# The last 1024 tokens' projection moved into the first windows of the attention, and the first maxima beside the sixth group

## The reference

```python
xn = _layernorm(x)                                   # (1, 4096, 256)
Q, K, V = heads(xn @ W_Q), heads(xn @ W_K), heads(xn @ W_V)   # 16 heads of 16
scores = einsum('bhqd,bhkd->bhqk', Q, K) / 16 ** 0.5 + causal
out = einsum('bhqk,bhkd->bhqd', softmax(scores), V) ... @ W_o
x = x + out + ffn(xn)     # scores of 16 experts by gate_w, each takes its best 512 tokens,
                          # gelu(Wg x) * (Wu x) @ Wd, times the weight, added up; and a shared expert
```

## Time and profile before

| | |
|---|---|
| median of 3 runs | 2411.45 us (2410.39 to 2411.78) |
| profiled execution | 2411.44 us, its span 2409.7 us |
| PE busy | 2318.2 us, 96% |
| DVE busy | 1927.6 us, 80% |
| ACT busy | 1493.8 us, 62% |
| units' reductions on DVE (L954) | x2176, 1292.9 us |
| mean granted clock of TensorE | 0.974 |

### The profile page before, as it was taken

One profiled execution on the slowest core, in us unless ns is written; L12 is line 12 of the kernel. 1 busy time (PEld: TensorE's weight loads), 2 busy tenths in 40 slices (PEclk: granted clock), 3 DMA queues, 4 the chain that ended last, 5 costly groups with the idle time before them and its releaser, 6 DMA issues. The chain is left out here.

```text
span 2409.7 us, 52756 instructions
## 1 busy us (share of the span) xinstructions
PE 2318.2 (96%) x20269; PEld 1504.9 (62%) x20275; DVE 1927.6 (80%) x3721; ACT 1493.8 (62%) x2901; POOL 241.9 (10%) x228
## 2 busy tenths in 40 slices
PE   7987999999999999999999999998998999999997
PEld 4554555555555555555545555557887888888886
DVE  6776999999999898999999999865744666666664
ACT  2233677788877777888788877773223555455543
POOL 3000000000000000000002000001120232323232
PEclk9956999999999999999999999999999999999999
DMA  7854000003100004200001000002243444444444
GB/s 262 321 154 89 17 10 8 6 11 63 28 3 11 18 14 90 42 17 13 3 9 41 4 4 4 30 7 84 71 159 104 109 136 136 107 112 135 137 104 115
DMA packets 141914, 167.97 MB, mean 70 GB/s; under 512 B 53612, under 2 KB 107372, under 8 KB 141628
## 3 DMA queue, kind: packets, MB, share of 16 engines
q1 hardware_dynamic: 127916, 142.87, 19.4%
q0 software_dynamic: 13728, 22.28, 5.0%
q10 hardware_dynamic: 64, 0.02, 0.0%
HBM read 117.86 MB, written 48.56 MB: 69 GB/s over the span
## 5 line engine op out<-in xcount | busy, mean ns | idle before, releaser
L954 DVE TENSOR_REDUCE a_mp<-a_pm 128x1 f32<-128x512 f32 (+3 forms) x2176 | 1292.9, 673 | 78.3 <-PE a_pm L1121 54.2
L1079 ACT ACTIVATE a_p<-a_ps 128x512 f32<-128x512 f32 (+2 forms) x2176 | 1121.3, 587 | 373.5 <-PE a_ps L1202 266.0
L1224 PE MATMUL a_po<-a_p,a_v 128*32 128x384 f32 (+2 forms) x8688 | 615.1, 386 | 0.9
L1121 PE MATMUL a_pm<-a_k,a_qr 48*128 48x512 f32 (+3 forms) x1152 | 418.2, 459 | 3.1 <-ACT p_xs L379 1.2
L1202 PE MATMUL a_ps<-a_qr,a_k 50*128 50x512 f32 (+3 forms) x1152 | 390.0, 435 | 21.4 <-DMA a_qr<-a_nb 21.4
L1121 PE MATMUL a_pm<-a_k,a_q 48*128 48x512 f32 (+3 forms) x1152 | 405.0, 435 | 5.2
L1202 PE MATMUL a_ps<-a_q,a_k 50*128 50x512 f32 (+3 forms) x1152 | 372.8, 423 | 1.0 <-ACT a_p L1079 0.8
L1224 PEld LDWEIGHTS a_po<-a_p,a_v 128*32 128x32 f32 x8688 | 202.7, 109 | 202.3 <-issue 134.3
L1202 PEld LDWEIGHTS a_ps<-a_qr,a_k 50*128 50x128 f32 x1152 | 192.7, 192 | 198.1 <-ACT a_p L1079 143.4
L1202 PEld LDWEIGHTS a_ps<-a_q,a_k 50*128 50x128 f32 x1152 | 185.5, 185 | 185.0 <-ACT a_p L1079 161.2
L1644 ACT ACTIVATE e_g<-e_pg 128x512 f32<-128x512 f32 x128 | 76.5, 598 | 243.7 <-PE e_pu L1722 243.7
(11 more groups left out here) (177 smaller groups left out, 2052.8 us busy)
## 6 DMA issues: line engine op xcount, KB each, us to landing
e_wgu<-in_wg SPq DMA_DIRECT2D x18, 1024.0 KB, 5.6
e_wgu<-in_wu SPq DMA_DIRECT2D x18, 1024.0 KB, 7.6
e_wd<-in_wd SPq DMA_DIRECT2D x18, 1024.0 KB, 10.2
q_parts<-p_parts SPq DMA_DIRECT2D x16, 512.0 KB, 5.9
k_parts<-p_parts SPq DMA_DIRECT2D x16, 512.0 KB, 7.0
a_k<-k_parts SPq DMA_DIRECT2D x60, 128.0 KB, 3.4
a_q<-q_parts SPq DMA_DIRECT2D x96, 64.0 KB, 2.3
a_qr<-q_parts SPq DMA_DIRECT2D x84, 64.0 KB, 2.4
```

Source lines behind the costliest of these rows:

```text
L954: eng.tensor_reduce(mp[:, i, heads[0]:heads[-1] + 1, r, kc], ps[:, 0:len(heads) * w].rearrange("p (a n) -> p a n", n=w), AX.X, ALU.max).th ...
L1079: eng.activation(pr[:, i, heads[0]:heads[-1] + 1, off:GT], pS[n % HEADS][:, 0:len(heads) * w].rearrange("p (a n) -> p a n", n=w), ACT.Exp) ...
L1121: last = eng.matmul(ps[:, n * w:(n + 1) * w], QT[t % SLOTS][tile, a, r * P:(r + 1) * P], KT[g % 2][tile, a, kc * GT:kc * GT + w], start=n ...
L1224: last = eng.matmul(pO[h * VW:(h + 1) * VW, lo:hi], V[TILES[t][0] % 2][:, b, h * VD:h * VD + VW], PR[blk % PBUF][:, h, lo:hi], start=b == ...
```

## The change

The products of groups 6 and 7 (tokens 3072 to 4095) leave the projection. They become jobs in the windows: `latev` (a value block) and `late` (a product m), which use the banks a_pm in turn with the units. The values of group 6 stand in window 0, its products in windows 1 to 4, the values of group 7 in windows 5 and 6, its products in windows 7 to 10. Group 7 is still normalised and turned, beside group 5, into banks of pQ. Tile 0's units stand beside group 5, in four parts, with its maxima as the last; nothing else is held back (13 instead of 25). `windows()` gets one empty window ahead (LEAD). SP issues tile 0's maxima beside the last product of group 5, and ACT those of tiles 1 to 3 (OWN), which SP did. SP loads tiles 2 and 3 before it stores the late products, tiles 4 to 7 after that. The buffers a_p are used in reversed order, and ACT waits for the stores of the parts only at the fourth block.

```diff
         def tensor(eng, beside):
...
-                group(NG // 2 - 1, s, s == 0, beside)
+                group(NG // 2 - 2, s, True, beside if s else None)
+            eng.wait_ge(s_lo, 4 * (NG - 2) + 2)
+            turn(NG - 1, 1, pQ)
...
+        def late_products(eng, g, m, ps):
+            eng.wait_ge(s_xs, 2 * (g + 1) + 2)
+            for d in range(DC):
+                last = eng.matmul(ps[:, :], WQK[:, m // 2, d, (m % 2) * P:(m % 2 + 1) * P], XS[g % 2][:, d, :],
+                                  start=d == 0, stop=d == DC - 1)
+            return last
...
+        def late_high(eng, g, m, ps):
...
+            eng.mul(LATE[g % 2][m][:, 0, :], ps[:, :], 0.25 if m < 2 else 1.0).then_inc(front.s_lhi, 1)
+
+        def late_low(eng, g, m, ps):
+            eng.wait_ge(front.s_lhi, 4 * (g - NG + 2) + m + 1)
+            return eng.scalar_tensor_tensor(out=LATE[g % 2][m][:, 1, :], in0=ps[:, :], scalar=0.25 if m < 2 else 1.0,
...
-        SIZES = [3, 3, 3, 3, 4, 3, 3, 3]
+        SIZES = [3, 3, 3, 4]
+        LEAD = 1
+        LATER = {0: [("latev", NG - 2, t) for t in range(4)],
+                 5: [("latev", NG - 1, t) for t in range(2)], 6: [("latev", NG - 1, t) for t in range(2, 4)]}
+        for m in range(4):
+            LATER[1 + m], LATER[7 + m] = [("late", NG - 2, m)], [("late", NG - 1, m)]
...
-            out, issued, blk, pv, col, pause = [], {}, 0, 0, skipped(0), PAUSE
+            out, issued, blk, pv, col, pause = [([], [])] * LEAD, {}, 0, 0, skipped(0), PAUSE
...
+                for u in late:
+                    row.append(u)
+                    count = 2 if u[0] == "latev" else 4
+                    row += us[:count]
+                    us = us[count:]
...
-                project_sync(eng)
-                front.ahead(eng, 2)
+                project_sync(eng, lambda eng: store_max(eng, 0))
+                for n in range(2, 4):
+                    front.ahead(eng, n)
+                for g in range(NG - 2, NG):
+                    eng.wait_ge(s_mf, BANKS + AT["latev", g, TG - 1] + 1)
+                    front.late_store_values(eng, g)
+                    for m in range(4):
+                        eng.wait_ge(s_mf, BANKS + AT["late", g, m] + 1)
+                        front.late_store(eng, g, m)
                 front.stored(eng)
-                front.tables(eng)
-                for n in range(3, SLOTS):
+                front.stored_values(eng)
+                eng.wait_ge(front.s_lst, 128)
+                for n in range(4, SLOTS):
                     fetch_q(n)
                     fetch_kv(eng, 0, n)
-                    if n == 3:
-                        store_max(eng, 1)
+                front.tables(eng)
...
-                store_max(eng, 0)
-                front.stored(eng)
...
+                        elif u[0] == "late":
+                            eng.wait_ge(s_mb, AT[u] + 1)
+                            front.late_high(eng, *u[1:], pM[AT[u] % BANKS])
+                    for t in range(1, OWN + 1):
+                        if IN["max", t] == w - 1:
+                            store_max(eng, t)
```

More of the change, by code:

```diff
@@ L263, in group @@
                 for m in range(4):
+                    if beside and m == 3:
+                        beside(eng)
                     wait_alone(k, eng, s_lo, 4 * g + m + 1 + 4)
@@ L274, in sync @@
                     group(i, s, True, True)
-            for n in range(NG - 4, NG):
-                group(n // 2, n % 2, n + 3 < NG, n + 2 < NG)
+            for n in range(NG - 4, NG - 2):
+                group(n // 2, n % 2, n + 3 < NG, n + 2 < NG, beside if n == NG - 3 else None)
+            for n in range(NG - 2, NG):
+                tokens(n, n % 2)
         def gpsimd(eng):
@@ L352, in vector, with group @@
             norm(0, 1)
-            with eng.Fori(0, NG // 2 - 1) as i:
-                for s in range(2):
[L355 to L360, removed]
+            def group(i, s, beside=None):
+                g = 2 * i + s
+                values(i, s)
+                eng.wait_ge(s_tr, g + 1)
+                eng.wait_ge(s_tab[s], 16 * i + 16)
+                norm(i + 1, s)
+                rest(i, s, beside)
+            with eng.Fori(0, NG // 2 - 2) as i:
+                for s in range(2):
+                    group(i, s)
             for s in range(2):
-                values(NG // 2 - 1, s)
-                rest(NG // 2 - 1, s, beside)
+                group(NG // 2 - 2, s, beside if s else None)
         def scalar(eng):
@@ L398, in scalar, with tensor @@
             for s in range(2):
-                group(NG // 2 - 1, s, s == 0, False)
-        def tensor(eng, beside, room):
+                group(NG // 2 - 2, s, True, True)
+            rows(NG // 2 - 1, 1, pQ)
+        def tensor(eng, beside):
             eng.sem_inc(s_xs, 2)
@@ new lines, in late_values @@
+        def late_values(eng, g, t, ps):
+            eng.wait_ge(s_xs, 2 * (g + 1) + 2)
+            for d in range(DC):
+                last = eng.matmul(ps[:, 0:D + E], XS[g % 2][:, d, t * P:(t + 1) * P], WVG[:, d, :],
+                                  start=d == 0, stop=d == DC - 1)
+            return last
+        def late_high(eng, g, m, ps):
+            if m == 0 and g == NG - 2:
+                eng.wait_ge(s_pst[0], 64 * (NG // 2 - 1) + 64)
+            if m == 0 and g == NG - 1:
+                eng.wait_ge(s_xn, NG)
+                eng.wait_ge(s_tr, NG)
+                for s in range(2):
+                    eng.wait_ge(s_tab[s], 16 * (NG // 2))
+            eng.mul(LATE[g % 2][m][:, 0, :], ps[:, :], 0.25 if m < 2 else 1.0).then_inc(front.s_lhi, 1)
@@ L775, in plan @@
                       for items, pieces in WINDOWS]
+            for w, ls in LATER.items():
+                length[w] += sum(1800 if u[0] == "late" else 900 for u in ls)
             at = [sum(length[:w]) for w in range(n + 1)]
@@ L808, in attend @@
         FIRST, LISTS = plan()
-        BESIDE = {(NG - 2 + n // 4, n % 4): FIRST[sum(SIZES[:n]):sum(SIZES[:n + 1])] for n in range(8)}
+        BESIDE = {(NG - 3, n): FIRST[sum(SIZES[:n]):sum(SIZES[:n + 1])] for n in range(4)}
         SOFT = BEGIN[2 * NQ - 1]
@@ L818, in stream @@
                 us, row = [u for u in ls if u[0] == "unit"], []
+                late = [u for u in ls if u[0] in ("late", "latev")]
                 for blk, _ in items:
@@ L829, in stream @@
                         tile = u[5]
+                for u in late:
[3 more added lines that the diff above has]
+                    us = us[count:]
                 row += us
                 row += [("piece", *piece) for piece in pieces]
-                row += [u for u in ls if u[0] != "unit"]
+                row += [u for u in ls if u[0] != "unit" and u not in late]
                 out.append(row)
```

95 lines of the change are left out of this document (67 added, 28 removed).

## The result

The changed kernel takes 2406.02 us (median of 20 runs, 2386.34 to 2448.49), the one before 2413.49 us in the same 20 rounds (2410.36 to 2417.73). The ratio is 0.9958, 95% interval 0.9938 to 0.9978: faster by 0.4%, 7.5 us by the medians and 10 by the ratio where 31.8 were forecast, and outside the range by 7 us. Runs more than 1.5% above the fastest of their kernel are left out of every ratio (4 of these 20, further down 4 of 6 of e1_fill and 1 of 12 of f2_early_rows0), and the medians are of all runs. What strikes first is the spread, 62 us where the kernel before has 7. It goes with the clock: with the time at half clock taken as 2 x (1 - mean granted clock) x span, the fastest run (clock 0.987) has 62 us of it and the slowest (0.955) 220 us, and a line through all 20 is 2366 us + 0.36 x that time, correlation 0.99.

The account below looks back on a forecast made before the run. DVE's row maxima bound the kernel; idle DVE up to tile 3's maxima falls from 48.8 us to 3.8 + 8.0 + 2.7 + 0.5 + 2 = 17.0, a gain of 31.8, giving 2379.5 us. Range 2364 to 2399.

Parts of the forecast that it names:

- rival 2: Clock falls for a part after a new PE wait over some 3.5 us; gain about 16, 2395 us; chance 0.17.
- both holes: PE's waits for the first maxima of tiles 0 and 2: 10.01 us to 134.28 and 11.42 us to 208.46.
- three signs of being wrong: 0.50 clock beyond a few microseconds before 200 us; fourth a_nb CAST later than 215 us; time won given back later.
- The bound and the common point: DVE's row maxima bound the attention; both programs match at tile 3's maxima, 238.37 us before, and only shift behind it.
- Tile 0 beside group 5: Tile 0's maxima run beside group 5, PE-bound with 3.8 us of idle DVE, ending near 102.3 us.
- First score: PE reaches tile 0's first score at about 108 us without the earlier wait: 0 us, bounds 0 and 3.
- Eight late products: Products of groups 6 and 7 share four banks: 1.0 us of idle DVE each, 8.0 us together, bounds 3 and 14.
- ACT's issues: ACT instead of SP issues maxima of tiles 1 to 3; the 11.42 us PE wait goes, costing 0.5 us, bounds 0 and 2.
- SP late: SP's later loads delay storing tile 0's result, which DVE's tile 2 row needs: 2 us, bounds 0 and 8.
- Rival 3: Half clock from the first score to tile 3's maxima, 15.4 us later than before: 2427 us; chance 0.05.
- Rival 1: Clock holds and the shared banks give no stall: idle 3.8 + 2.7, gain 42, 2369 us; chance 0.08.
- Rival 4: Idle moves into new waits, SP's chain 8 us late with clock lost, stalls at upper bound: 2406 to 2416; chance 0.06.

Follow-up runs that it names:

- e1_fill: Changed kernel with one dense bf16 128x512 product of ones ahead of each unit in windows up to tile 6's first; 2850.6 us.
- f2_early_rows0: Changed kernel with tile 0's maxima behind the sixth group's fourth product, tiles 1 to 3's three units later, tile 0's result store ahead of 42 loads; 2393.4 us.
- e6_inject: e2_kvlate plus five extra DVE reduces ahead of the first unit of tile 5's fourth window, making PE wait once; 2392.1 us.
- a0_again: The changed kernel run once more, unedited; 2397.1 us.
- f3_latefirst: Changed kernel with late second-key-buffer loads, tile 0's maxima behind the sixth group's fourth product, tiles 1 to 3's three units later, late products first in their windows; 2380.0 us.
- f1_rows0: Changed kernel with one statement moved: the store of tile 0's result ahead of the second key buffer's 42 loads; 2384.6 us.
- e2_kvlate: Changed kernel with the second key buffer's 42 loads issued one group a window, from the second window behind tile 4's first score; 2388.0 us.
- e4: e2_kvlate with tile 0's maxima behind the sixth group's fourth product (m3) instead of ahead of it; 2384.6 us.

## Why the prediction was wrong

**The step that failed** is in "The change part by part" and in rival 2: that the clock falls only behind a wait "over some 3.5 us", so that with both holes closed it would read 1.00 from 88 to 230 us. That size came from a single row, the gap of 3.54 us. The trace after shows falls behind 2.54, 0.82, 1.83, 0.82 and 1.50 us, and e6_inject made one with 2.25 us. I had priced the waits of 1 us behind late products at their own length alone; they had the clock at stake. Of my three signs of being wrong two came: 0.50 for more than a few microseconds before 200 us, and time given back later. The third, the mark behind 215 us, was missed by less than a microsecond.

Point by point:
- *The bound and the common point*: right. From 290 us DVE works 48.86 of 51. But "everything behind it shifted as a whole" was wrong: 24.1 us at that mark, 1.1 at the last one. The sum stopped at a mark behind which I had found "the one for tile 3 ... costs as little".
- *Tile 0 beside group 5*: forecast to end at 102.3 us; its last low part starts at 102.71. Right in size, with a clock fall in it that I had not seen.
- *First score*: forecast about 108 us, no hole; measured 109.55, no wait. Right.
- *Eight late products*: 0.98 us at full clock, as forecast 1.0, but 3.72 at half clock. All eight together came to 18.3 us of idle DVE (11.9, 4.0 and 2.4 for p_parts, p_x and p_xn in the groups by line), not 8.0, and 4.3 above the bound of 14. The bound took a product as 1.98 us whatever the clock.
- *ACT's issues*: tiles 1 and 2 right. Tile 3's, issued till 217.9 us, let the score start only at 226.8 beside the loads: 1.5 us of wait, 3.6 in f2_early_rows0.
- *SP late*: the mechanism right, and the need within a microsecond (forecast 21.5 us behind the common point, 22.2 in a0_again). The chain came 4 us later than forecast (by the same 2.7 us for the landing at 25.0 instead of 21.2), because SP took 56.0 us for its loads (180.26 to 236.24) and not 51.3. The wait of 3.28 us lies in the bounds of 0 to 8. That the wait also costs the clock was rival 2's, and the larger sum.
- *The sum*: idle DVE to the common point 126.00 - 98.86 = 27.1 us. Of the forecast 17.0 only 15.0 belong there, since SP's 2 us lie behind it; 10.3 of the 12.1 too many are in the late products. DVE's own work to that point, taken over as 101.2 us, was 98.9. The forecast time itself is met by f3_latefirst, 2380.0 against 2379.5, but that is another program, with late loads and another order.

**Rival 2** ("the clock falls for a part", 0.17) named the place and the mechanism. It priced one fall of 40 us of DVE work and three blocks, a gain of 16; a0_again had a gain of 14 and the first series of 7.5; both profiles have five falls. *Rival 3* (half clock throughout) did not come. *Rival 1* had no support: where the clock held, the 0.98 us stalls were there. *Rival 4* (0.06, 2406 to 2416) has the first series' median at its lower end, and in kind it came nearest: the stalls were above their upper bound and the clock was lost, though SP's chain was 4 us late and not 8.

**What stays open.** Most short waits are passed without a fall (f1_rows0 and e6_inject passed one of 2.5 us at 99, where the changed kernel, a0_again and e2_kvlate fell), some falls stand behind waits of only 0.45 to 0.6 us (e4 at 121, f1 at 165) or 0.3 (f3 at 128 and 162), e1_fill fell without any, and a rise came after 3 to 31 us in the short falls and after 44 to 68 us in the long ones of the new order, with PE busy all the while in these. Which of two like waits is followed by a fall, and what ends a fall, no run here tells. Why the same kernel took 2406 us in one series and 2397 in the other is the same question.

## What to carry to other kernels

Put a mark that both programs pass in the same state, but read it at several places down to the end: a gain at the first of them is not yet a gain. Where narrow products run at full clock, a wait of PE of a microsecond or two is priced with the clock that it may cost, here up to 22 us (62 us at 0.36). Dense filler was no cure. Giving PE something independent to do behind each dense job (another order of the same work) went with the least time at half clock (12 us) and the best median, but its worth by itself isn't shown. When a queue's chain comes out as late as its need, move the one small store or load that others wait for ahead of the bulk: here one moved statement was worth 12 us, and its four runs lie within 4 us where six of the same kernel without it lay within 23.

## What the runs showed of the hardware

- The granted clock fell to 1.2 GHz behind waits of PE of 0.82 to 2.54 us in the profile after (0.3 to 3.6 us in all), and in 228 to 290 us stayed there through 62 us of PE without a gap. In this kernel a microsecond at half clock cost 0.36 us.
- Dense bf16 products of 128 rows between the narrow ones did not keep the full clock (e1_fill: 0.67 on average over 433 us of busy PE).
- A score that waits for its four small DMAs started 1.2 us after their issue in the earlier trace rows and 4.1 us in the earlier trace rows, but 8.9 us after it beside the 42 loads, in the profile after (217.9 to 226.8) and in f2_early_rows0 (214.4 to 223.4), at DMA shares of 1.1 to 1.2.
